# Single-head attention layers with the sources on the partitions, in groups of five destination blocks

## The chip, the cores and the metric
The kernel runs as one program on one core of a Trainium2 chip. The metric is the device time of one execution in microseconds. The core has a matrix engine (TensorE, PE in the profile), a vector engine (VectorE, DVE), a scalar engine (ScalarE, ACT), a general one (GpSimd, POOL), and queues that issue DMAs (SyncE, SP, above all). Each engine works through its own instructions in order and waits on semaphores for the others. SBUF and PSUM have 128 partitions; PSUM has eight banks of 2 KB a partition.

## The reference
A network over 3125 nodes of 256 features and 103125 edges (self loops among them): an attention layer of 8 heads of 32 columns, a mixture of experts, three single-head attention layers of 256 columns one after the other, and a last block that routes a part of the nodes. Each part adds to the node features. The three layers matter most here:

```python
def gat_conv(x, src, dst, W, a_src, a_dst, b):
    h = x @ W
    s = h @ a_src
    d = h @ a_dst
    alpha = jax.nn.leaky_relu(s[src] + d[dst], NEG_SLOPE)
    m = jax.ops.segment_max(alpha, dst, num_segments=n)
    ex = jnp.exp(alpha - m[dst])
    denom = jax.ops.segment_sum(ex, dst, num_segments=n)
    w = ex / (denom[dst] + 1e-16)
    out = jax.ops.segment_sum(h[src] * w[:, None], dst, num_segments=n)
    return out + b
x = jax.nn.gelu(gat_conv(x, src, dst, W1, as1, ad1, b1), approximate=False)
x = jax.nn.gelu(gat_conv(x, src, dst, W2, as2, ad2, b2), approximate=False)
x = jax.nn.gelu(gat_conv(x, src, dst, W3, as3, ad3, b3), approximate=False)
```

## The kernel before
The edge list is first turned into a dense mask in HBM, `mask_dram`, with a row for each destination and a column for each source: a large number where there is no edge, and otherwise what the count of equal edges adds to the score. From then on attention is dense. The nodes are 25 blocks of 128 (the last has 53), scores are kept negated, so that a maximum is a minimum, and everything is 4-byte floats.

The stages follow each other with no overlap: edges and mask (to 449 us), `heads_phase` (L821, to 1836), routing and experts (to 2316), `node_project_phase` (L1053, to 2366), `layers_phase` (L1229, to 3520), the last block. No planner and no scheduler orders the instructions: the order on an engine is the order of the code, and hand-offs are semaphore counts written by hand.

The heads run 200 units, one for each of 4 heads, 25 blocks and 2 passes. A unit is: DVE makes the scores of 128 destinations against 3125 sources (L978) and adds the mask with a running minimum (L982); ACT takes the exponentials in two halves, with their sums (L915); PE turns the 25 tiles of 128x128 so that sources lie on the partitions (L1014); ACT copies them from PSUM in four parts (L924); PE multiplies them with the sources' features (L1028). At a block's end ACT copies the sums out (L930), PE folds them (L1035), and ACT scales four pieces of 32 columns (L939) into the rows that POOL stores.

`node_project_phase` normalises the nodes and makes a table `hx` for the first layer (features of the sources and the two attention terms a node), and `el`, the source terms as a row on all partitions, plain and times 0.2.

The layers do for each destination block the same as a head's unit, with 256 columns: scores (L1309), mask and minimum (L1313), exponentials (L1487), 25 transposes (L1536), copies (L1496), 25 products with the stationary turned tile and 256 moving columns (L1547). Each turned tile waits for ACT's copy, each copy for PE's transposes, both with two buffers. A block behind, DVE divides by the sum and adds the bias (L1362), ACT takes the gelu (L1501), and for the next layer PE turns the row (L1557), projects it (L1566) and spreads its source term (L1574). The masks of the blocks come in one by one through two buffers on SP's queue (L1288), each when DVE is done with the one two blocks before.

Of the kernel before, what the change touches and what calls it, by code (L numbers as in the profile page):

```python
# [12 lines left out]
P = 128  # L13
# [399 lines left out]
def diagonal(g, first, rows, cols):  # L413

    flat = g["mask_dram"].rearrange("a b -> (a b)")
    start = first * (NS + 1)
    return flat[start:start + rows * cols * (NS + 1)].rearrange("(r q s) -> r q s", q=cols, s=NS + 1)[:, :, 0:1]
# [403 lines left out]
def heads_phase(nc, g, hx, el, mask, sc_first, nm, x1):  # L821

    with ExitStack() as ctx:
# [12 lines left out]
        psO = [ctx.enter_context(nc.psum_tensor(f"hd_psO{i}", [P, 512], F32)) for i in range(3)]  # L836
# [5 lines left out]
        s_mask = [sem(f"s_mask{i}") for i in range(2)]  # L842
        s_store = [sem(f"s_store{i}") for i in range(3)]
# [13 lines left out]

        @block.sync
        def _(sp):
            load_el(sp, 0, HG - 1, 0)  # L860
            load_el(sp, 0, HG - 1, 1)
            for B in range(2, BLOCKS):
                sp.wait_ge(s_nm, (B - 1) * HG)
                b = B % NB
# [4 lines left out]
                if b == 0:  # L869
                    for h in range(HG):  # L870
                        sp.wait_ge(s_lk, (B - 1) * HG + h + 1)
                        load_el(sp, B // NB, h, 0)
                        load_el(sp, B // NB, h, 1)

        @block.gpsimd
        def _(pool):
# [19 lines left out]
            for B in range(BLOCKS):  # L896
                q, b = B // NB, B % NB
                if B + 1 < BLOCKS:
                    halves_added(B + 1)
                pool.wait_ge(s_y, B + 1)  # L900
# [7 lines left out]
        def _(act):  # L908
# [17 lines left out]
            def copy_sums(B):  # L926
# [3 lines left out]
                nc.scalar.activation(oT[:, :, :].rearrange("p h n -> p (h n)"), psO[B % 3][:, 0:HG * P], ACT.Copy).then_inc(s_oT, 1)  # L930

            def rows(B):
                i = B % 3
                act.wait_ge(s_yT, B + 1)
                act.wait_ge(s_rd, B + 1)
                if B >= 3:
                    act.wait_ge(s_store[i], 16 * (B // 3))
                for h in range(HG):
                    last = nc.scalar.activation(y[:, i, h * CH:(h + 1) * CH], psY[:, h * CH:(h + 1) * CH], ACT.Copy,  # L939
                                                scale=rden[:, i, h:h + 1])  # L940
                last.then_inc(s_y, 1)

            exps(0, 0)
            exps(0, 1)
            for u in range(UNITS):
# [6 lines left out]
                for gi in range(4):  # L952
# [49 lines left out]
        def _(pe):  # L1002
# [14 lines left out]
            def products(n):  # L1017
# [3 lines left out]
                if gi == 0 and h == 0 and B >= 3:  # L1021
                    pe.wait_ge(s_y, B - 2)
                c0 = (B // NB * HG + h) * CH
                for t in range(TG[gi]):
# [3 lines left out]
                    last = nc.tensor.matmul(psO[B % 3][cg * CH:(cg + 1) * CH, h * P:(h + 1) * P], hx[0:r, tt, c0:c0 + CH],  # L1028
# [1247 lines left out]
```

## Time and profile before

| | us |
|---|---|
| Median of three runs | 3707.16 (3706.19 to 3713.21) |
| Profiled execution | 3711.51 |
| Its span in the profile | 3709.8 |
| PE busy in the span | 3419.7 |
| DVE busy | 2807.1 |
| ACT busy | 2515.5 |
| POOL busy | 316.0 |

The span is the time between the first and the last instruction that the profile shows of one execution. Busy times of an engine are sums over its instructions; instructions that follow each other closely overlap a little in the records, so that the distance of two starts says more of a price than a duration does. What the whole span hides, the stretches of the stages show.

### The profile page before, as it was taken

Reading aid. Unit: us, or ns where it says so; the run is one execution under the profiler, and the core shown is the slowest. Engines: PE = TensorE matmul, PEld = TensorE weight load, DVE = VectorE, ACT = ScalarE, POOL = GpSimd, SP = SyncE. Lnnn points to the kernel's source line nnn. Section 1 sums busy time; section 2 is a strip of 40 time slices with the busy share of each in tenths; the row PEclk is TensorE's granted clock in tenths of the full one; section 3 lists DMA queues with packets and bytes.
Section 4 is the critical chain, followed back from the end, with each engine's and each line's share of the span. In section 5 each row is a group of like instructions: output and inputs, shape, how many; then the busy total and the mean of one; then the engine's idle time right before and its main releaser. Section 6 shows DMA issues by size and latency. Waiting matters only on the chain. (4 is left out here: it accounts for less than half of the span.)

```text
span 3709.8 us, 69967 instructions
## 1 busy us (share of the span) xinstructions
PE 3419.7 (92%) x27369; PEld 2683.6 (72%) x27370; DVE 2807.1 (76%) x4237; ACT 2515.5 (68%) x4068; POOL 316.0 (9%) x280
## 2 busy tenths in 40 slices
PE   6999989999999999999769998799999999999999
PEld 4565566666666666666568998688878888888777
DVE  7999999999999999999652222766555565677594
ACT  5999899999999999999610111466656665676532
POOL 1000011010010010100004444000000000000000
PEclk9999999999999999999869999899999999999999
DMA  5433321121124211211268885322223221433101
GB/s 158 164 108 140 127 67 61 56 73 56 58 87 170 70 59 56 73 56 58 59 192 257 238 229 122 139 105 105 105 88 113 105 105 61 175 114 113 36 15 35
DMA packets 144871, 390.36 MB, mean 105 GB/s; under 512 B 20048, under 2 KB 91550, under 8 KB 126750
## 3 DMA queue, kind: packets, MB, share of 16 engines
q1 hardware_dynamic: 120520, 346.56, 26.7%
q0 software_dynamic: 20816, 36.07, 5.0%
q8 instruction: 224, 3.67, 0.4%
q10 hardware_dynamic: 3206, 3.20, 0.4%
q14 instruction: 105, 0.86, 0.1%
HBM read 327.87 MB, written 61.11 MB: 105 GB/s over the span
## 5 line engine op out<-in xcount | busy, mean ns | idle before, releaser
L924 ACT ACTIVATE hd_probsT<-hd_psT 128x768 f32<-128x768 f32 (+1 forms) x800 | 660.4, 852 | 70.2 <-PE hd_psT L1014 70.1
L1028 PE MATMUL hd_psO<-hd_probsT,hx 128*32 128x128 f32 (+1 forms) x10000 | 571.8, 281 | 129.1 <-ACT hd_probsT L924 129.0
L1547 PE MATMUL ly_psO<-hx_a,ly_probsT 128*128 128x256 f32 x2500 | 584.0, 381 | 0.0
L1028 PEld LDWEIGHTS hd_psO<-hd_probsT,hx 128*32 128x32 f32 (+1 forms) x10000 | 317.3, 108 | 322.6 <-ACT hd_probsT L924 216.0
L1496 ACT ACTIVATE ly_probsT<-ly_psT 128x768 f32<-128x768 f32 (+1 forms) x300 | 248.6, 829 | 393.6 <-PE ly_psT L1536 393.6
L1547 PEld LDWEIGHTS ly_psO<-hx_a,ly_probsT 128*128 128x128 f32 x2500 | 454.0, 189 | 71.4 <-issue 16.6
L1014 PE MATMUL hd_psT<-ident,hd_scores 128*128 128x128 f32 (+1 forms) x3325 | 478.9, 281 | 0.0
L978 DVE SCALAR_TENSOR_TENSOR hd_scores<-el_heads,hx 128x3125 f32<-128x3125 f32 x133 | 460.9, 3465 | 0.0
L982 DVE CUSTOM_DVE_ANT_0 hd_scores<-hd_scores,mask_heads 128x3125 f32<-128x3125 f32 x133 | 453.6, 3411 | 5.7
L915 ACT ACTIVATE hd_scores<-hd_scores,negmax 128x1664 f32<-128x1664 f32 (+1 forms) x266 | 430.1, 1617 | 5.4 <-DVE negmax L982 5.4
L1014 PEld LDWEIGHTS hd_psT<-ident,hd_scores 128*128 128x128 f32 (+1 forms) x3325 | 355.4, 141 | 98.9 <-issue 98.9
L1547 PE MATMUL ly_psO<-hx_b,ly_probsT 128*128 128x256 f32 x1250 | 292.7, 382 | 0.0
L489 DVE TENSOR_SCALAR onehot_c<-iotaC,stage_c 128x392 bf16<-128x392 f16 x1176 | 289.9, 316 | 0.0
L1536 PE MATMUL ly_psT<-ident,ly_scores 128*128 128x128 f32 x1875 | 258.2, 276 | 16.6 <-ACT ly_scores L1487 16.6
L2008 ACT ACTIVATE moe_hidden<-moe_ps_h 128x512 f32<-128x512 f32 x64 | 38.2, 597 | 331.7 <-PE moe_ps_h L1973 331.7
L1487 ACT ACTIVATE ly_scores<-ly_scores,ly_negmax 128x1664 f32<-128x1664 f32 (+1 forms) x150 | 239.3, 1595 | 22.0 <-DVE ly_negmax L1336 11.4
L1547 PEld LDWEIGHTS ly_psO<-hx_b,ly_probsT 128*128 128x128 f32 x1250 | 227.4, 190 | 35.8 <-issue 8.3
L1313 DVE CUSTOM_DVE_ANT_0 ly_scores<-ly_scores,ly_mask 128x3125 f32<-128x3125 f32 x73 | 248.9, 3410 | 3.1
L1014 PE MATMUL hd_psT<-ident,scores 128*128 128x128 f32 (+1 forms) x1675 | 243.1, 283 | 8.7 <-ACT scores L915 8.7
L1536 PEld LDWEIGHTS ly_psT<-ident,ly_scores 128*128 128x128 f32 x1875 | 221.2, 142 | 40.5 <-ACT ly_scores L1487 17.2
L1973 PEld LDWEIGHTS moe_ps_h<-moe_xT,moe_w 128*128 128x128 f32 x2048 | 241.5, 194 | 5.6 <-DVE moe_xT L2014 2.2
L1973 PE MATMUL moe_ps_h<-moe_xT,moe_w 128*128 128x128 f32 x2048 | 241.8, 277 | 1.6 <-DVE moe_xT L2014 1.6
(348 smaller groups left out, 5037.7 us busy)
## 6 DMA issues: line engine op xcount, KB each, us to landing
ly_mask<-mask_dram SPq DMA_DIRECT2D x72, 1568.0 KB, 6.6
moe_w<-in_L_ffn_w SPq DMA_DIRECT2D x144, 512.0 KB, 5.0
mask_heads<-mask_dram SPq DMA_DIRECT2D x46, 1568.0 KB, 6.7
mask_dram<-el_heads SPq DMA_DIRECT2D x196, 196.0 KB, 1.9
el_heads<-el_dram SPq DMA_DIRECT2D x5, 1568.0 KB, 9.7
el_heads<-el_slope_dram SPq DMA_DIRECT2D x5, 1568.0 KB, 13.1
x<-x SPq DMA_DIRECT2D x8, 640.0 KB, 8.4
el_heads<-el_dram POOLq DMA_DIRECT2D x3, 1568.0 KB
```

Of the source, the lines that this page charges most:

```text
L489: last = nc.vector.tensor_scalar(oc[:, k, :], g["iotaC"][:, :], c[:, k:k + 1], None, ALU.is_equal)
L915: nc.scalar.activation(sc[u % 3][:, halves[j]], sc[u % 3][:, halves[j]], ACT.Exp, scale=-1.0, bias=nm[:, u % 3:u % 3 + 1], accum_out=den[: ...
L924: nc.scalar.activation(pT[:, gi % 2, 0:w], psT[gi % 2][:, 0:w], ACT.Copy).then_inc(s_ev, 1)
L978: nc.vector.scalar_tensor_tensor(sc[c][:, :], el[:, h, 0, 0:N], hx[:, b, o:o + 1], el[:, h, 1, 0:N], ALU.subtract, ALU.min).then_inc(s_lk, 1)
L982: nc.vector.tensor_tensor_reduce(out=sc[c][:, :], in0=sc[c][:, :], in1=mask[:, B % 2, 0:N], scale=1.0, scalar=3.0e38, op0=ALU.add, op1=ALU ...
L1014: last = nc.tensor.transpose(psT[gi % 2][0:r, t * P:(t + 1) * P], sc[u % 3][:, c0:c0 + r], g["ident"][:, :])
L1028: last = nc.tensor.matmul(psO[B % 3][cg * CH:(cg + 1) * CH, h * P:(h + 1) * P], hx[0:r, tt, c0:c0 + CH], pT[0:r, gi % 2, t * P:(t + 1) * P ...
L1313: nc.vector.tensor_tensor_reduce(out=sc[:, c, :], in0=sc[:, c, :], in1=mask[:, B % 2, 0:N], scale=1.0, scalar=3.0e38, op0=ALU.add, op1=ALU ...
L1496: nc.scalar.activation(pT[:, gi % 2, 0:w], psT[gi % 2][:, 0:w], ACT.Copy).then_inc(s_ev, 1)
L1536: last = nc.tensor.transpose(psT[gi % 2][0:r, t * P:(t + 1) * P], sc[:, B % 3, c0:c0 + r], g["ident"][:, :])
L1547: last = nc.tensor.matmul(psO[B % 2][:, 0:D], pT[0:r, gi % 2, t * P:(t + 1) * P], hx[B // NB % 2][0:r, tt, 0:D], start=tt == 0, stop=tt == ...
L1973: last = nc.tensor.matmul(out[:, m * P:(m + 1) * P], w12[:, t % WS, i, k, m * P:(m + 1) * P], xT[:, t % 2, k, :], start=k == 0, stop=k == 1)
```

## The change
In the layers, scores are made with the sources on the partitions in the first place, so nothing is turned behind the exponentials. Five destination blocks form a group (640 columns). A group is 13 steps of two source tiles. In a step, DVE makes the scores of each tile from two rows that stand on all partitions (`rw`, one number a destination) and the tile's source term on the partitions (L1493), and adds a tile of the mask that lies turned in HBM, `maskT_dram` (L1503); ACT takes the exponentials (L1642); PE multiplies each 128x128 piece with the table, 257 columns, into the five PSUM banks of the five blocks (L1767). Column 0 of the table is 1, so that the sum of the weights falls out of the product. Four step buffers lie between DVE and PE (`RING`).

The maximum of a destination, needed before its scores can be shifted, comes from a pass over the untouched mask and `el` (L1510), one for each block of the next group, at the steps `at_step`; then a few short operations (`shifts`), spreads on PE (L1785) and copies on ACT (L1668) make the next group's two rows. At a group's end ACT drains the five banks (L1654) behind the exponentials of the next group's second step; DVE's division and ACT's gelu follow at its fourth; the former group's blocks are turned, projected and spread one by one between the products. In the layers' last group this is done after the last product, over all PSUM banks. In the last layer POOL adds the rows that DVE added before.

The heads turn the mask on the way: a quarter block a unit, three or four transposes on PE (`turn_mask`), a copy on ACT, a store by SP. One 128-column copy and a POOL multiplication take the place of ACT's four scaled pieces. The router's stage stores the diagonal to both masks and makes four weight columns more. The projection stage reads five masks (two before), and makes the first group's minima.

In the diff, `nm`, `sc` and the like are buffers, `s_...` semaphores.

```diff
 # heads
+            def store_turned(j):
+                sp.wait_ge(s_mc, j + 1)
+                sp.dma_start(g["maskT_dram"][...], mt[...]).then_inc(s_mst[j % 2], 16)
             for B in range(2, BLOCKS):
+                for h in range(HG - 1):
+                    store_turned((B - 2) * HG + h)
                 sp.wait_ge(s_nm, (B - 1) * HG)
+                sp.wait_ge(s_mT, (B - 1) * HG)
                 sp.dma_start(mask[0:r, B % 2, :], g["mask_dram"][b * P:b * P + r, :]).then_inc(s_mask[B % 2], 16)
...
-                for h in range(HG):
-                    last = nc.scalar.activation(y[:, i, h * CH:(h + 1) * CH], psY[:, h * CH:(h + 1) * CH], ACT.Copy,
-                                                scale=rden[:, i, h:h + 1])
+                nc.scalar.activation(y[:, i, :], psY[:, 0:P], ACT.Copy).then_inc(s_raw, 1)
...
+                    if gi == 3 and u + 2 < UNITS:
+                        copy_mask(u + 2)
                     if gi % 2 == 1 and u + 1 < UNITS:
                         exps(u + 1, gi // 2)
...
+                if n % 4 == 1 and n // 4 + 2 < UNITS:
+                    turn_mask(n // 4 + 2)
 # layers
+            def load_turned(C):
+                if C >= RING:
+                    sp.wait_ge(s_msk, C - RING + 1)
+                sp.dma_start(mT[0:r, s, 0:len(ks), 0:w], g["maskT_dram"][...])
+            for C in range(LAYERS * STEPS):
+                load_turned(C)
+                for B in fetch.get(C, ()):
+                    load_mask(B)
+            def scores(C):
+                if C >= RING:
+                    multiplied(dve, C - RING)
+                if c == 0:
+                    dve.wait_ge(s_row, spreads_upto(G) + SPREADS[G % NG])
+                for i, k in enumerate(tiles(c)):
+                    last = nc.vector.scalar_tensor_tensor(pb[0:r, s, i, 0:w], rw[0:r, G % 2, 0, 0:w], hx[l % 2][0:r, k, N8:N8 + 1],
+                                                          rw[0:r, G % 2, 1, 0:w], ALU.add, ALU.min)
+            def masked(C):
+                dve.wait_ge(s_mT[s], 16 * (C // RING) + 16)
+                nc.vector.tensor_tensor(pb[0:r, s, 0:n, 0:w], pb[0:r, s, 0:n, 0:w], mT[0:r, s, 0:n, 0:w], ALU.add)
+        at_step, first_steps = (0, 1, 2, 3, 5), (1, 2, 3, 5, 6)
+                    for c in range(NCK):
+                        if gi and c == 0:
+                            masked(C - 1)
+                        scores(C)
+                        if c:
+                            masked(C - 1)
+                        if gi + 1 < NG:
+                            maxima(first_of(G + 1) + d, G + 1)    # at its step
+                        if gi and c == 3:
+                            rows(G - 1)
 # ACT
+                        exps(G * NCK + c)
+                        if gi and c == 1:
+                            drain(G - 1)
+                        if gi and c == 3:
+                            gelus(G - 1)
 # PE, products of a step
+                pe.wait_ge(s_ex, C + 1)
+                for i, k in enumerate(tiles(c)):
+                    for d in range(size(G)):
+                        if k == 0 and G and d < size(G - 1):
+                            pe.wait_ge(s_dr, first_of(G - 1) + d + 1)
+                        nc.tensor.matmul(psO[d][0:m, 0:D + 1], pb[0:r, s, i, d * P:d * P + m], hx[l % 2][0:r, k, 0:D + 1], ...)
```

PE in the heads, one unit (`hd_psT` turned scores, `hd_psO` sums, `hd_psM` turned mask). Before:

```order
L1014 MATMUL hd_psT<-ident,hd_scores 128x128 x6
L1028 MATMUL hd_psO<-hd_probsT,hx 32x128 x6
L1014 MATMUL hd_psT<-ident,hd_scores 128x128 x5
L1014 MATMUL hd_psT<-ident,hd_scores 53x128
L1028 MATMUL hd_psO<-hd_probsT,hx 32x128 x6
```

And now:

```order
L1057 MATMUL hd_psT<-ident,hd_scores 128x128 x6
L1071 MATMUL hd_psO<-hd_probsT,hx 32x128 x6
L1089 MATMUL hd_psM<-ident,mask_heads 128x128 x3
L1057 MATMUL hd_psT<-ident,hd_scores 128x128 x5
L1057 MATMUL hd_psT<-ident,hd_scores 53x128
L1071 MATMUL hd_psO<-hd_probsT,hx 32x128 x6
```

The three mask tiles come between a unit's second products and its last transposes.

DVE in the first layer, one destination block of before (`ly_scores` scores, `ly_psX` and `ly_psH` the end of an earlier block):

```order
L1309 SCALAR_TENSOR_TENSOR ly_scores<-el,hx_a 128x3125
L1312 MEMSET ly_spare 1x1
L1313 ISA ly_scores,ly_negmax<-ly_scores,ly_mask 128x3125
L1313 ISA ly_negmax 128x1
L1317 TENSOR_SCALAR ly_has_edge<-ly_negmax 128x1
L1381 COPY x<-ly_psX 128x128
L1382 TENSOR_SCALAR x<-ly_psX 128x128
L1369 COPY ly_xT<-ly_psX 128x256
```

And now, from the last step of the first group to the third of the second (`probs` the four step buffers, `least` a block's minimum, `ly_mask` a mask by destinations):

```order
L1493 SCALAR_TENSOR_TENSOR probs<-ly_rows,hx_a 53x640
L1503 TENSOR_TENSOR probs<-probs,ly_mask_turned 128x1280
L1503 TENSOR_TENSOR probs<-probs,ly_mask_turned 53x640
L1493 SCALAR_TENSOR_TENSOR probs<-ly_rows,hx_a 128x640 x2
L1510 ISA ly_mask,least<-el,ly_mask 128x3125
L1510 ISA least 128x1
L1493 SCALAR_TENSOR_TENSOR probs<-ly_rows,hx_a 128x640 x2
L1503 TENSOR_TENSOR probs<-probs,ly_mask_turned 128x1280
L1510 ISA ly_mask,least<-el,ly_mask 128x3125
L1510 ISA least 128x1
L1493 SCALAR_TENSOR_TENSOR probs<-ly_rows,hx_a 128x640 x2
L1503 TENSOR_TENSOR probs<-probs,ly_mask_turned 128x1280
```

A new group's first scores are masked only behind the next step's scores and one minimum, its second step's behind two.

PE in the first layer, before, between one block's parts (`ly_psT` turned scores, `ly_psO` sums):

```order
L1536 MATMUL ly_psT<-ident,ly_scores 128x128 x7
L1547 MATMUL ly_psO<-hx_a,ly_probsT 128x256 x6
L1566 MATMUL ly_psH<-wx,ly_xT 128x258 x2
L1536 MATMUL ly_psT<-ident,ly_scores 128x128 x6
L1547 MATMUL ly_psO<-hx_a,ly_probsT 128x256 x7
L1574 MATMUL ly_psX<-ident,hx_b 128x128
```

And now in a group, around the spreads of the next group's rows (`ly_uv` to `ly_psR`):

```order
L1767 MATMUL ly_psO<-hx_a,probs 128x257 x30
L1796 MATMUL ly_psX<-ident,ly_sums 128x128 x2
L1767 MATMUL ly_psO<-hx_a,probs 128x257 x10
L1785 MATMUL ly_psR<-ident,ly_uv 128x128 x4
L1805 MATMUL ly_psH<-wx,ly_xT 128x260 x2
L1767 MATMUL ly_psO<-hx_a,probs 128x257 x10
L1796 MATMUL ly_psX<-ident,ly_sums 128x128 x2
L1815 MATMUL ly_psR<-ident,hx_b 128x128
```

Between products there are no turned scores any more, but the ends of the former group's blocks and the next group's rows.

## Rows read from the trace of the kernel before
**Rows 1.** Busy time of each engine by stretch; columns as in the first line
```profile
core 0: us, PE busy (x) PEld busy (x) DVE busy (x) ACT busy (x) POOL busy (x), PEclk, DMA share, GB/s
452.00:1830.00 1378.00, 1245.98 (x15400) 893.63 (x15400) 1354.88 (x846) 1296.26 (x1852) 127.51 (x104) 1.00 0.22 70
2372.00:3512.00 1140.00, 1124.85 (x6069) 960.33 (x6069) 701.71 (x1078) 708.16 (x832) 0.00 (x0) 0.99 0.30 104
2317.00:2333.00 16.00, 5.78 (x21) 4.42 (x22) 11.13 (x45) 1.83 (x6) 0.00 (x0) 0.54 1.03 358
2760.00:2765.00 5.00, 2.58 (x6) 1.37 (x5) 2.15 (x10) 0.44 (x1) 0.00 (x0) 0.50 0.00 0
2770.00:2775.00 5.00, 5.00 (x22) 4.23 (x22) 4.96 (x4) 2.47 (x4) 0.00 (x0) 0.79 0.55 176
```
**Rows 2.** The page's costliest groups, heads: busy us, mean ns | idle before, releaser
```profile
L924 ACT ACTIVATE hd_probsT<-hd_psT 128x768 f32<-128x768 f32 (+1 forms) x800 | 660.4, 852 | 70.2 <-PE hd_psT L1014 70.1
...
L978 DVE SCALAR_TENSOR_TENSOR hd_scores<-el_heads,hx 128x3125 f32<-128x3125 f32 x133 | 460.9, 3465 | 0.0
L982 DVE CUSTOM_DVE_ANT_0 hd_scores<-hd_scores,mask_heads 128x3125 f32<-128x3125 f32 x133 | 453.6, 3411 | 5.7
```
**Rows 3.** Timeline of DVE, heads and end of layers: start us, duration us
```profile
1001.73 3.41 DVE L982 CUSTOM_DVE_ANT_0 scores<-scores,mask_heads 128x3125 f32<-128x3125 f32 x1
...
1005.07 3.47 DVE L978 SCALAR_TENSOR_TENSOR hd_scores<-el_heads,hx 128x3125 f32<-128x3125 f32 x1
...
1008.58 3.41 DVE L982 CUSTOM_DVE_ANT_0 hd_scores<-hd_scores,mask_heads 128x3125 f32<-128x3125 f32 x1
...
3517.54 0.42 DVE L1416 SCALAR_TENSOR_TENSOR ly_y<-hx_b,ly_y 128x256 f32<-128x256 f32 x1
3517.88 0.42 DVE L1418 TENSOR_TENSOR x<-x,hx_b 128x256 f32<-128x256 f32 x1
```
**Rows 4.** Timeline of PE in the first layer, one block and a bit
```profile
2712.40 3.19 PE L1547 MATMUL ly_psO<-hx_a,ly_probsT 128*128 128x256 f32 x14
...
2716.30 2.75 PE L1547 MATMUL ly_psO<-hx_a,ly_probsT 128*128 128x256 f32 x12
2718.89 0.82 PE L1536 MATMUL ly_psT<-ident,ly_scores 128*128 128x128 f32 x6
...
2726.00 1.14 PE L1566 MATMUL ly_psH<-wx,ly_xT 128*128 128x258 f32 x4
2726.98 0.82 PE L1536 MATMUL ly_psT<-ident,ly_scores 128*128 128x128 f32 x6
2727.63 1.68 PE L1547 MATMUL ly_psO<-hx_a,ly_probsT 128*128 128x256 f32 x7
```
**Rows 5.** Waits of the layers: us in total, times, longest us
```profile
ACT ly_probsT L1496 <- PE ly_psT L1536: 393.6, 162, 3.6
```
**Rows 6.** Timeline of ACT in the heads and behind the last layer
```profile
1006.87 0.79 ACT L924 ACTIVATE hd_probsT<-hd_psT 128x768 f32<-128x768 f32 x1
1007.56 0.59 ACT L930 ACTIVATE hd_sumsT<-hd_psO 128x512 f32<-128x512 f32 x1
1008.03 0.81 ACT L924 ACTIVATE hd_probsT<-hd_psT 128x768 f32<-128x768 f32 x1
...
3512.34 1.28 ACT L1507 ACT_TABLE_LOAD   x1
```
**Rows 7.** Timeline of PE where the second layer follows the first
```profile
2755.70 1.14 PE L1566 MATMUL ly_psH<-wx,ly_xT 128*128 128x258 f32 x4
...
2766.38 3.03 PE L1536 MATMUL ly_psT<-ident,ly_scores 128*128 128x128 f32 x13 [3.29 <-ACT ly_scores L1487]
2769.21 4.66 PE L1547 MATMUL ly_psO<-hx_b,ly_probsT 128*128 128x256 f32 x14
```
**Rows 8.** POOL's sums in the heads: duration ns min/median/max
```profile
L887 POOL TENSOR_TENSOR hd_rden<-hd_den x50: 191/1700/3411, 474.5 to 1820.4; 128x4 f32<-128x4 f32 x50
```
**Rows 9.** The page's DMA issues: KB each, median us to landing
```profile
ly_mask<-mask_dram SPq DMA_DIRECT2D x72, 1568.0 KB, 6.6
```

More of the change, by code:

```diff
@@ L410, with diagonal @@
 LOOP_STEPS = -(-L1_LOOPS // DL)
[L413 to L415 removed]
+def diagonal(g, first, rows, cols, of="mask_dram"):
+    flat = g[of].rearrange("a b -> (a b)")
     start = first * (NS + 1)
@@ L1151, in _ @@
                 normalise(b)
-                if b > second.start:
-                    copy_h(b - 2)
-            copy_h(NB - 2)
-            copy_h(NB - 1)
-            dve.wait_ge(s_first_masks, 32)
+            dve.wait_ge(s_first_masks, 16 * len(places))
+            for i in range(len(PIECES)):
+                maxima(i)
+            n = len(places)
+            for i in range(1, len(PIECES)):
+                dve.wait_ge(s_least, (i + 1) * n)
+                c.wait()
+                c(nc.vector.tensor_tensor(qp[:, 0, :], qp[:, 0, :], qp[:, i, :], ALU.min))
+            c.wait()
+            c(nc.vector.tensor_copy(q[:, 0, 0:n], qp[:, 0, :]))
+            c.wait()
+        @block.gpsimd
+        def _(pool):
+            for table in tables:
+                nc.gpsimd.memset(table[:, :, 0:1], 1.0).then_inc(s_one, 1)
+            pool.wait_ge(s_one, len(tables))
         @block.scalar
@@ L1260, in layers_phase @@
-        ends = [min(e, NB) for e in LAST_GROUPS]
-        group_of = lambda e: range(ends[ends.index(e) - 1] if e != ends[0] else 0, e)
-        turned, upto = [], 0
-        for b in range(NB):
-            ready = max([e for e in ends if e + 2 <= b], default=0)
-            turned.append(range(upto, min(upto + 2, ready)))
-            upto = turned[-1].stop if turned[-1] else upto
-        late = range(upto, NB)
-        LAG = 4
-        added = [range(0) if b < LAG else range(LAG) if b == LAG else range(b - 1, b) for b in range(NB)]
@@ new lines, in layers_phase @@
+        tiles = lambda c: range(c * KC, min(c * KC + KC, NB))
+        depth = lambda k: min(P, N - k * P)
+        spreads_upto = lambda G: G // NG * sum(SPREADS) + sum(SPREADS[:G % NG])
+        place, user, landed = {}, {}, {}
+        latest, loads = [None] * len(masks), [0] * len(masks)
+        for B in range(LAYERS * NB):
+            if B < SIZES[0]:
+                s = B
+            elif B % NB in (2, 3):
+                s = B % NB
+            elif B % NB == SIZES[0] - 1:
+                s = UPPER
+            else:
+                s = 0 if latest[1] > latest[0] else 1
+            place[B], user[B] = s, latest[s]
+            latest[s] = B
+            loads[s] += 0 if B < SIZES[0] else 1
+            landed[B] = loads[s]
@@ new lines, in spread_rows @@
+            def spread_rows(G, j):
+                pe.wait_ge(s_uv, G + 1)
+                bank = psR if G % NG else psO[j]
+                if G % NG:
+                    pe.wait_ge(s_row, spreads_upto(G) + j)
+                if spread["el"]:
+                    pe.wait_ge(s_ec, spread["el"])
+                spread["rows"] += 1
+                for d in range(2 * j, min(2 * j + 2, size(G))):
+                    for i in range(2):
+                        o = (d - 2 * j) * 2 * P + i * P
+                        last = nc.tensor.matmul(bank[:, o:o + P], uv[:, G % 2, i, d:d + 1].broadcast_to([P, P]), g["ident"][:, :],
+                                                start=True, stop=True)
+                last.then_inc(s_sp, 1)
```

842 lines of the change are left out of this document (502 added, 340 removed).

## The prediction
> **What bounds the kernel now.** I read the busy time by stage first [rows 1]. In the heads stage (452 to 1830) DVE is busy 1354.88 of 1378 us, ACT 1296.26, PE 1245.98; in the layers stage (2372 to 3512) PE is busy 1124.85 of 1140, DVE and ACT some 705 each. So two stages with two limits. In the heads the page's groups confirm it: DVE's two passes over 3125 columns (L978, L982) stand idle 0.0 and 5.7 us in all, while ACT's copies of turned scores (L924) waited 70.2 us for PE [rows 2]. One head of one block costs DVE 3.34 + 3.51 = 6.85 us start to start [rows 3], and 199 of them are the stage. In the layers the waits show the reverse: ACT stood 393.6 us waiting for PE's transposes [rows 5]. One destination block there takes 2727.63 - 2712.40 = 15.23 us on PE without a gap [rows 4]. Of it, 25 products at 0.432 (each two instructions; 12 start within 2.59) are 10.8, 25 transposes at 0.109 (6 within 0.65) 2.7, and the end of a block (projection 0.98, two pairs of small transposes at 0.22) 1.42.
>
> **Heads.** Each unit gains three or four mask transposes on PE (0.11 each, 0.4), and on ACT a copy of 384 or 512 columns. ACT's prices start to start: 768 columns 0.69, 512 columns 0.47, so 0.86 ns a column and 384 cost 0.36 [rows 6]. ACT gives back four small scaled copies a block for one of 128 columns (some 0.8 to 0.15 a block, an estimate by the same line), 0.16 a unit. Net +0.22 on ACT. Its idle time was (70.2 + 5.4) / 199 = 0.38 a unit, and the new copy stands right before the exponentials whose following copies had that wait, so PE catches up in its shadow. DVE stays the limit: no change in cadence. If nothing of the wait is absorbed, ACT's unit is 6.85 + 0.22 - 0.1 at most, +22 us over the stage: rival C. The mask turning of units 0 and 1 delays PE's start some 2 us, but DVE needs the first unit's transposes only two units (13.7 us) later. The new stores (196 KB a unit) meet a stage whose DMA share is 0.22 [rows 1]. SP's mask loads now queue behind three stores of the block before; they have a block's 27 us for 6.6 us [rows 9]. The POOL multiplication of the last rows lies on the end: +1. I take +2, between 0 and 22.
>
> **Node projection and router.** The router's eight more tiny ACT copies and the second diagonal store lie beside waits: 0 (0 to 3). In the projection two masks become five, 7.8 MB at the 358 GB/s that 2317 to 2333 shows [rows 1]: 22 us, landed before the tables end. Five minima in four pieces are 5 x 3.34 plus 15 starts; only the last piece (two blocks, five short instructions) and the joins of 0.15 lie behind the last table: +4 (2 to 10). The layers give it back: they no longer begin with 6.85 us of DVE passes and an exponential of 1664 columns, but with four tiny DVE steps, ten spreads and three copies (5 us) and a first step (6 us). Equal.
>
> **Layers: work.** A group of five blocks is 13 steps. On PE a step is ten products, 4.34; a group 125 x 0.434 = 54.25, ten row spreads 2.2, five block ends 7.1: 63.5, against 5 x 15.23 = 76.2. All 25 transposes a block and ACT's copies behind them are gone. In the last layer blocks have no projection (15.23 - 1.42 + 0.22 = 14.03); 70.2 becomes 57.6. So PE alone would win 12.6 in 15 groups, 189 us.
>
> **Layers: what is late next.** DVE by its own starts: 256 columns 0.34, 3125 columns 3.34, thus 1.046 ns a column [rows 3]: 640 cost 0.74, 1280 cost 1.41. A step is 2 x 0.74 + 1.41 = 2.89; a step that also holds a block's minimum 6.23, more than PE's 4.34. A group is 13 steps (36.8), five minima (16.7), shifts and rows (3): 56.5 of PE's 63.5, so in the mean DVE keeps up, but the order matters. I added these durations in program order, with four slots between DVE and PE, 1.16 for two exponentials and 0.05 to 0.2 a hand-off:
> - First group: five steps with a minimum. PE waits 1.9 in steps 1 to 3, 0.5 and 2.8 in steps 5 and 6: 9.
> - Into the second group: its scores wait for rows spread after step 10. Then DVE does 1.48 + 3.34 + 1.48 + 1.41, ACT two exponentials, DVE 3.34 + 1.48 + 1.41, ACT two more, and only then (it stands behind the second exponentials) the drain that PE's first product waits for: about 15.5, of which PE covers steps 11 and 12 and little else. Behind the drain on ACT stand the exponentials of step 2, which PE does not want before it is through steps 0 and 1. PE waits 10, then 2.6 in the minima steps.
> - Into the third and fourth the rows come a step earlier and block ends fill PE: 3.1 + 1.5 each. Into the fifth, without minima: 2.2.
> Sum 33. PE works 5 x 63.5 less the last group's spreads and ends, 306: first to last product 339. Before: 25 x 15.23 less the last block's absent transposes, 378. Gain 39 in each of two layers. In the last layer there are fewer block ends to fill PE, boundaries cost 6.8 in place of 3.1, stalls 44 on 284: 328 against 348, gain 20.
>
> **Layer change.** Before, from the last projections (2755.70) to the next first product (2769.21) 13.5 us [rows 7]. After: drain 0.6, five rows 1.5, a table load 1.28 (row at 3512.34 [rows 6]), gelus to 4.6, five block ends at 1.31 of PE in a chain over ACT to 14.2, the last piece, joins and shifts 3, rows 4, first step 6: 27. Twice 13.5 lost. The tail has five blocks instead of one behind the last product: +3 (2 to 6).
>
> **Clock.** At the change before, the granted clock was 0.50 at 2760 to 2765 and still 0.79 at 2770 to 2775 [rows 1], and 14 products from 2769.21 are 4.66 long where 14 from 2712.40 are 3.19 [rows 4, 7]. Stalls of 10 us into three second groups and the longer changes should cost 2 to 3 each at 1.2 GHz: +8 (0 to 30, if the 3 us stalls do it too).
>
> **Sum.** Layers -(39 + 39 + 20) + 27 + 3 + 8 = -60; heads +2; projection +4. The profiled execution took 3711.51 (span 3709.8), so 3657; it lies 4.35 over the median 3707.16, so I forecast 3652.
>
> **Rivals.**
> A, the forecast: PE-bound with stalls at the group boundaries. Own range 3620 to 3690.
> B, fewer stalls: if half of the 110 us of stalls (33 + 33 + 44) is not there, because the four buffers cover more than my walk lets them: 3597. For it: DVE's mean is below PE's. Against: the boundary chain is a chain of data.
> C, the heads go over to ACT: 3652 + 20 = 3672. For it: ACT's margin is 0.38 - 0.22 a unit. Against: the wait it replaces.
> D, slower: late masks. In the layers SP now loads 655 KB of turned mask (rows of 2560 B) a step, and in the same queue the 1568 KB masks of the next group. Of blocks 3 to 5 of a group, each mask can start only when DVE has left the buffer two minima before, and is wanted 9.1 us later (6.23 + 2.89). In that time 2.2 MB must land; with 2 us of latency that asks 315 GB/s. The mean need is 16 MB in 65 us, 250 GB/s. Rows show 358 with 1 KB rows and 6.6 us for a mask alone [rows 1, 9], so it holds; below 315 it decides. At 200 GB/s a group's 16 MB take 81 us, 17 more than PE, in 15 groups: +250, and at 250 GB/s each of those three steps is some 3 late, +135 less what the stalls hide (half): 3720. That is the slower side.
> E, POOL against DVE. POOL's 50 small sums in the heads took 191 ns at best, 1700 in the median and 3411 at most [rows 8], the last one being the length of L982, and DVE's two passes have the same means with or without them. The change adds 50 multiplications of 128 columns in the heads and moves 50 additions of 256 to POOL in the last layer. If each held DVE for 0.4 us, twice POOL's shortest, the time would be 3652 + 40 = 3692. The Trainium skill ("SBUF — State Buffer", section "SBUF: two separate sides") says that a DVE operation with two SBUF inputs and a GpSimd operation that reads SBUF lock a shared port in turn for a whole instruction. By that rule the trace's waits of POOL agree (3411), but no row shows DVE paying, so it is a rival and no term.
>
> **Numbers.** A 0.58, B 0.10, C 0.10, D 0.14, E 0.08. Outcomes within 0.2% (7.4 us) cannot be told from no change. Faster than 3699.7: A but for 0.02, B, C and most of E, 0.80; same 0.06; slower 0.14, D. The range reaches to B below and to D's near end above: 3595 to 3715.
>
> **What would show it.** In the profile after: DVE's pair L1021 and L1025 in the heads still 6.85 apart and ACT's waits for PE below 70 us (C: DVE idle on turned scores). In the layers PE steps of 4.34, ACT hardly ever waiting for PE, PE waiting for exponentials most in the first product of second groups (about 10 us) and in first groups, DVE waiting for rows; no DVE wait of over 1 us for the masks (else D); DMA at 230 GB/s or more; some 27 us between layers with the clock at 0.50. Wrong if groups take 75 us or more, or if the heads grow by over 10.

## The result, and the profile after
The changed kernel took 3773.00 us (median of four, 3770.76 to 3776.33) against 3707.91 before: 65 us or 1.8% more by the medians; the ratio of the runs is on record as 1.0166, with an interval of 1.0144 to 1.0188. Forecast were 3652, with 3595 to 3715 as the range: wrong by 121 us, and on the other side of the kernel before. The profiled execution has a span of 3774.6 us, 64.8 more than before.

The first DMA issues of the stages show where the span went. The view is SP's timeline of the changed kernel; columns are start, length of a run of issues, and what they move.

```profile
1846.76 0.37 SPq L689 DMA_DIRECT2D gate_w<-in_L_ffn_gate_w  x1
...
2333.43 4.35 SPq L1151 DMA_DIRECT2D x<-x  x5
...
2389.54 1.54 SPq L1427 DMA_DIRECT2D ly_bias<-in_L_gnn_b  x3
...
3585.48 0.37 SPq L2326 DMA_DIRECT2D mod_w<-in_L_ffn_w  x1
```

| Stage | before | after | forecast |
|---|---|---|---|
| up to the end of the heads | 1836.6 | 1846.8 (+10.1) | +2 |
| routing and experts | 479.0 | 486.7 (+7.7) | 0 |
| node projection | 50.7 | 56.1 (+5.4) | +4 |
| layers | 1153.9 | 1195.9 (+42.0) | -60 |

Routing and experts run the same code but for the second diagonal and twelve small copies. From the first of the experts' 128 weight loads to the next stage it was 386.4 us before, 393.1 after, and 384.7 to 403.1 in the eleven runs below, which all leave it as it is. So these 7 us lie within the scatter of the profiled executions. The heads and above all the layers carry the error.

In the layers PE no longer stands at its limit. Busy time by layer, from the first to the last product (columns as in [rows 1]):

```profile
2403.50:2781.60 378.10, 338.68 (x1490) 275.00 (x1490) 274.02 (x289) 138.46 (x247) 0.00 (x0) 0.92 0.60 208
2811.30:3182.40 371.10, 335.12 (x1490) 272.50 (x1490) 272.38 (x289) 138.67 (x248) 0.00 (x0) 0.93 0.59 203
3212.20:3572.00 359.80, 311.25 (x1370) 249.84 (x1370) 290.77 (x361) 149.21 (x240) 51.18 (x40) 0.93 0.56 189
```

Where before PE was busy 1124.85 of 1140 at a granted clock of 0.99 [rows 1], it is now busy some 0.9 of each layer (0.87 in the last), at 0.92 or 0.93. The layers are 378, 371 and 357 long (the third window runs 2.9 us past the last product); forecast were 339, 339 and 328. ACT, which waited 393.6 us for PE [rows 5], now waits for DVE. The waits of the layers (total us, times, longest):

```profile
ACT probs L1642 <- DVE probs L1503: 299.7, 85, 12.0
...
PE ly_psO L1767 <- ACT probs L1642: 76.3, 25, 8.6
PE ly_psO L1767 <- ACT ly_sums L1654: 67.6, 12, 10.2
...
DVE ly_mask L1518 <- ACT el L1686: 35.4, 3, 14.2
DVE ly_mask L1518 <- ACT x L1686: 33.1, 3, 11.6
DVE ly_mask L1510 <- DMA ly_mask<-mask_dram: 28.6, 4, 9.0
```

The third row is the boundary between groups as the walk had it: twelve waits, longest 10.2, 67.6 in all; the forecast adds up to some 65 (63 to 66, as the last layer's fifth group is read). The last three rows are waits of DVE; but for those of the last piece at each layer change, the walk did not have them. They are where the search began. Two of them on DVE's timeline, in the fourth group of the first layer and at the fourth step of the fifth:

```profile
2629.72 1.48 DVE L1503 TENSOR_TENSOR probs<-probs,ly_mask_turned 128x1280 f32<-128x1280 f32 x1
2640.16 3.42 DVE L1510 CUSTOM_DVE_ANT_0 ly_mask<-el,ly_mask 128x3125 f32<-128x3125 f32 x1 [8.96 <-DMA ly_mask<-mask_dram]
...
2703.28 1.33 DVE L1503 TENSOR_TENSOR probs<-probs,ly_mask_turned 128x1130 f32<-128x1130 f32 x1
2716.17 2.16 DVE L1518 CUSTOM_DVE_ANT_0 ly_mask<-x,ly_mask 128x1920 f32<-128x1920 f32 x1 [11.55 <-ACT x L1686]
```

And PE's timeline around the end of that fourth group shows a difference of price:

```profile
2694.06 4.50 PE L1767 MATMUL ly_psO<-hx_a,probs 128*128 128x257 f32 x20
2698.40 1.04 PE L1805 MATMUL ly_psH<-wx,ly_xT 128*128 128x260 f32 x4
...
2710.44 4.96 PE L1767 MATMUL ly_psO<-hx_a,probs 128*128 128x257 f32 x20
2715.33 0.49 PE L1815 MATMUL ly_psR<-ident,hx_b 128*128 128x128 f32 x2
2715.66 4.97 PE L1767 MATMUL ly_psO<-hx_a,probs 128*128 128x257 f32 x20
2724.94 1.65 PE L1767 MATMUL ly_psO<-hx_a,probs 128*128 128x257 f32 x3 [4.31 <-ACT probs L1642]
```

A step of the fourth group starts 4.34 us before what follows it, as forecast; in the fifth group it is 4.89, with the granted clock at 1.00 (2702 to 2712) and nothing waited for. The last row's wait of 4.31 is the 11.55 us of DVE, come through the four buffers.

### The profile page after: what moved, and what is told of

It is laid out like the page before. It is cut to its first block and busy times, and to the rows that moved or that the text cites. A ratio compares the mean times of both kernels' runs of the same rounds, so it can differ in the third digit from the quotient of the medians.

```text
span 3774.6 us, 68675 instructions
## 1 busy us (share of the span) xinstructions
PE 3381.0 (90%) x26419; PEld 2613.9 (69%) x26420; DVE 2994.5 (79%) x4222; ACT 2316.3 (61%) x4102; POOL 457.5 (12%) x382
## 5 line engine op out<-in xcount | busy, mean ns | idle before, releaser
L1767 PE MATMUL ly_psO<-hx_a,probs 128*128 128x257 f32 (+1 forms) x2500 | 607.1, 399 | 101.5 <-ACT probs L1642 52.0
L960 ACT ACTIVATE hd_probsT<-hd_psT 128x768 f32<-128x768 f32 (+1 forms) x800 | 662.3, 852 | 38.2 <-PE hd_psT L1057 37.9
L1767 PEld LDWEIGHTS ly_psO<-hx_a,probs 128*128 128x128 f32 (+1 forms) x2500 | 476.8, 196 | 214.3 <-ACT probs L1642 113.9
L1767 PE MATMUL ly_psO<-hx_b,probs 128*128 128x257 f32 (+1 forms) x1250 | 303.9, 399 | 42.7 <-ACT probs L1642 24.4
L1642 ACT ACTIVATE probs<-probs,hx_a 128x640 f32<-128x640 f32 (+3 forms) x250 | 189.9, 809 | 218.8 <-DVE probs L1503 218.6
L1493 DVE SCALAR_TENSOR_TENSOR probs<-ly_rows,hx_a 128x640 f32<-128x640 f32 (+3 forms) x250 | 212.7, 891 | 120.4 <-PE ly_psO L1767 81.1
L1767 PEld LDWEIGHTS ly_psO<-hx_b,probs 128*128 128x128 f32 (+1 forms) x1250 | 239.0, 197 | 96.7 <-ACT probs L1642 46.7
L1503 DVE TENSOR_TENSOR probs<-probs,ly_mask_turned 128x1280 f32<-128x1280 f32 (+3 forms) x195 | 274.0, 1411 | 1.7 <-DMA ly_mask_turned<-mask_turned_dram 1.7
L2261 ACT ACTIVATE moe_hidden<-moe_ps_h 128x512 f32<-128x512 f32 x64 | 38.2, 597 | 338.7 <-PE moe_ps_h L2226 255.1
L550 PE MATMUL cnt<-onehot_c,onehot_dst_a 128*128 128x392 bf16 x1176 | 232.1, 334 | 11.3 <-DVE onehot_c L489 11.0
L918 POOL TENSOR_TENSOR hd_rden<-hd_den 128x4 f32<-128x4 f32 x50 | 100.4, 2008 | 1127.0 <-ACT hd_scores L951 737.4
```

Of the source, the lines that this page charges most:

```text
L550: last = nc.tensor.matmul(o, ohA[:, s, :, k], ohC[:, s, k, :], start=k == 0 and not further, stop=True, skip_group_check=True)
L960: nc.scalar.activation(pT[:, gi % 2, 0:w], psT[gi % 2][:, 0:w], ACT.Copy).then_inc(s_ev, 1)
L1493: last = nc.vector.scalar_tensor_tensor(pb[0:r, s, i, 0:w], rw[0:r, G % 2, 0, 0:w], hx[l % 2][0:r, k, N8:N8 + 1], rw[0:r, G % 2, 1, 0:w], ...
L1503: nc.vector.tensor_tensor(pb[0:r, s, 0:n, 0:w], pb[0:r, s, 0:n, 0:w], mT[0:r, s, 0:n, 0:w], ALU.add).then_inc(s_msk, 1)
L1767: last = nc.tensor.matmul(psO[d][0:m, 0:D + 1], pb[0:r, s, i, d * P:d * P + m], hx[l % 2][0:r, k, 0:D + 1], start=k == 0, stop=k == NB - 1)
```

## The experiments
The theory from these rows: four separate causes, each visible in one of the rows above (the last block's narrow tiles, the late masks, the partial minima's wait, and DVE's two minima at a boundary). The rivals: one common limit (DVE's sum, the DMA, the clock). All runs are the changed kernel with one edit unless said otherwise; times are medians, against 3773.0; lengths of the layers stage against 1195.9. Two runs that leave the layers as they are have 1195.6 and, with PE kept busy, 1195.3.

**Full tiles in the last block.**

```diff
-                        m = min(P, w - d * P)
+                        m = P
```

> The last block of a layer has 53 destinations; here its products use all 128 columns of the stationary tile instead of 53 (the surplus sums belong to no node and are not used). In the changed kernel a step of the last group takes 5.0 us on PE and of the other groups 4.34. Theory (switching between a 128-column and a 53-column stationary tile costs PE time, two such tiles a step): the step falls to 4.34, 8 us in each of three last groups, 20 to 26 us in all, near 3749. Rival (the 565-column rows of that group are slow in themselves, or DVE sets the step): no change, 3773.

3749.87 us (3748.73 to 3751.27); layers 1174.5, 21.4 shorter. PE's timeline in the fifth group of the first layer:

```profile
2703.22 4.50 PE L1767 MATMUL ly_psO<-hx_a,probs 128*128 128x257 f32 x20
2707.55 0.38 PE L1815 MATMUL ly_psR<-ident,hx_b 128*128 128x128 f32 x2
2707.77 4.50 PE L1767 MATMUL ly_psO<-hx_a,probs 128*128 128x257 f32 x20
```

The step is back at 4.33. More columns in the stationary tile made the step cheaper, and the sums for nodes that don't exist cost nothing.

**Narrow tiles side by side.** Does the change between tile shapes cost, or the narrow tile?

```diff
-                for i, k in enumerate(tiles(c)):
-                    for d in range(size(G)):
+                pairs = [(i, k, d) for i, k in enumerate(tiles(c)) for d in range(size(G))]
+                narrow = lambda d: w - d * P < P
+                for i, k, d in sorted(pairs, key=lambda p: narrow(p[2])):
...
```

> The last group's two products a step with a 53-column stationary tile stand side by side at the end of the step instead of each behind four full ones. Theory (the cost is in changing between tile shapes): half as many changes, the step falls from 5.0 to 4.7 us, 4 us a layer, 3761. Rival (a product with 53 columns is slow in itself): the step stays at 5.0, 3773.

3760.49 us (3755.15 to 3763.01); layers 1184.9, 11.0 shorter. PE in the same place:

```profile
2709.81 4.63 PE L1769 MATMUL ly_psO<-hx_a,probs 128*128 128x257 f32 x20
2714.37 0.49 PE L1817 MATMUL ly_psR<-ident,hx_b 128*128 128x128 f32 x2
```

4.56 to the next instruction, where it was 4.89 and is 4.33 with full tiles: of the excess of 0.56 a step, 0.23 is left with half of the changes. That answers to the switching theory; two narrow tiles side by side are as narrow as before. The rows of the weight loads (PEld) show the changes themselves. In the changed kernel a step holds two such pairs of pauses, one into the narrow tile and one out of it:

```profile
2712.26 0.17 PEld L1767 LDWEIGHTS ly_psO<-hx_a,probs 128*53 128x53 f32 x2 [0.33 <-issue]
2712.83 1.60 PEld L1767 LDWEIGHTS ly_psO<-hx_a,probs 128*128 128x128 f32 x8 [0.40 <-issue]
```

With the narrow tiles side by side it holds one pair, and with full tiles none:

```profile
2713.37 0.61 PEld L1769 LDWEIGHTS ly_psO<-hx_a,probs 128*53 128x53 f32 x4 [0.33 <-issue]
2714.37 0.30 PEld L1817 LDWEIGHTS ly_psR<-ident,hx_b 128*128 128x128 f32 x2 [0.40 <-issue]
```

**The burst of masks later.** Three masks of the next layer, 4.7 MB, came in one burst at the start of the fourth group, ahead of the mask that DVE wanted next.

```diff
-                return (B // NB) * STEPS - 2 * NCK + 3
+                return (B // NB) * STEPS - 2 * NCK + 9 + B % NB - 2
```

> The three masks of the next layer's first group that SP loads in one burst (4.7 MB) at the start of the fourth group come 6 to 8 steps later. In the changed kernel DVE waited 9.0 and 7.9 us for a mask in just these two groups, and their length was 77 us against 69 of the group before. Theory (late masks, of my rival D, at this place only): these waits go and both groups fall by some 8 us, 16 in all, 3757. Rival (the masks are late because the queue is full all the time): the waits appear at another mask, 3773.

3750.48 us (3746.69 to 3755.38); layers 1174.7, 21.2 shorter, a little over the expected 16. The waits for masks:

```profile
DVE ly_mask L1510 <- DMA ly_mask<-mask_dram: 11.8, 2, 7.2
```

Two of four waits are gone, the two at the starts of the first and the last layer are left, and none came up elsewhere: the queue is not full, it was asked in the wrong order.

**Partial minima later.**

```diff
-                        elif l < LAST and c in range(3, 3 + 2 * SIZES[0], 2):
+                        elif l < LAST and c in (5, 7, 9, 11, 12):
...
```

> In the last group of the first two layers, DVE takes its partial minima for the next layer (1920 columns) at steps 5, 7, 9, 11, 12 instead of 3, 5, 7, 9, 11. In the changed kernel the first of them waited 11.6 us for a copy of source terms that PE makes only behind the products of step 1, and the masking of step 3 stands behind it. Theory: PE's stall of 4 us (and a clock drop) in step 3 of these two groups goes, 5 to 8 us each, 10 to 16 in all, near 3760. Rival (the four buffers already cover it, PE loses nothing): 3773.

3762.25 us (3761.26 to 3770.07); layers 1181.5, 14.4 shorter. PE runs 60 products' instructions without a gap where it stood 4.31 us before:

```profile
2722.78 14.97 PE L1767 MATMUL ly_psO<-hx_a,probs 128*128 128x257 f32 x60
```

**The drain earlier.**

```diff
-                        if gi and c == 1:
+                        if gi and c == 0:
                             drain(G - 1)
```

> ACT empties the five sums behind the first exponentials of the next group instead of behind the second, one DVE step (6.3 us) earlier. Theory (DVE's chain of scores, mask and minima sets the first steps of a group; the drain is only the visible end of it): PE starts a group up to 6.3 us earlier but then waits for exponentials in steps 1 to 5; 1 to 3 us in each of 12 boundaries, 10 to 35 in all, near 3750. Rival (the wait for the drain is the loss itself): 6.3 us in each second group and in the last layer's groups, 3 in the others, 55 or more, with the clock staying up: 3715.

3758.08 us (3755.79 to 3775.59); layers 1183.4, 12.5 shorter. The waits change their name:

```profile
PE ly_psO L1767 <- ACT probs L1642: 122.9, 36, 12.8
...
PE ly_psO L1767 <- ACT ly_sums L1654: 14.6, 11, 3.8
```

53 us less are waited for the drain, and 47 more for exponentials. So the drain was the end of DVE's chain more than a cause of its own: of 53 us, 12.5 were gained.

**No minima at a boundary.**

```diff
-        shift_step = lambda G: 6 if G % NG == 1 else 5
+        shift_step = lambda G: 6 if G % NG == 1 else 4
...
-                maxima_at[B] = ((G - 1) * NCK + (first_steps if G % NG == 1 else at_step)[d]) if G % NG else G * NCK
+                early = (8, 10, 12, 15, 17) if G % NG == 2 else (7, 9, 11, 15, 17)
+                maxima_at[B] = G * NCK if G % NG == 0 else (G - 1) * NCK + first_steps[d] if G % NG == 1 else (G - 2) * NCK + early[d]
...
```

> The minima of the third, fourth and fifth groups are spread: three of them in steps 7, 9, 11 (8, 10, 12 in the first group) of the group two before, two in steps 2 and 4 of the group before; their shifts one step earlier. So no minimum stands between a group's first scores and its drain. Theory (the two minima there are the stall at the boundary): 6.7 us less DVE in front of the drain; second groups 7, others 3 to 6 earlier, 35 to 45 us in all, near 3733. Rival (DVE's sum or the masks' landing sets the groups, wherever the minima stand): 10 at most.

3725.37 us (3717.53 to 3729.76); layers 1146.1, 49.8 shorter, more than expected. The waits for the drain halve, and of the four waits for masks two are left:

```profile
PE ly_psO L1769 <- ACT probs L1644: 60.9, 22, 9.1
...
PE ly_psO L1769 <- ACT ly_sums L1656: 34.4, 12, 4.4
...
DVE ly_mask L1511 <- DMA ly_mask<-mask_dram: 11.9, 2, 7.1
```

A mask is fetched by the step of the minima before it in its buffer (`fetch_at`), so this edit moved the loads too, and the two late masks of the fourth groups are gone here as they are with the later burst. So not all of the 49.8 is the boundary: from first product to first product, the two fourth groups gave 16 of it.

**PE kept busy at a boundary.**

```diff
+                        if gi and c == 0 and l < LAST:
...
+                            for _ in range((0, 64, 20, 20, 12)[gi]):
+                                nc.tensor.transpose(psX[:, 0:P], g["ident"][:, :], g["ident"][:, :])
                         products(G * NCK + c)
```

> Added work whose result is not used: 64 transposes (7 us at full clock) on PE while it waits at the start of a second group, 20 at the third and fourth, 12 at the fifth, in the first two layers. Theory (the low clock behind a stall costs little here, since DVE sets the first steps): the granted clock stays up at the boundary, 0 to 6 us gained, near 3770. Rival (the clock is the large loss): 2 to 3 us at each of eight boundaries, 16 to 24, 3753.

3772.36 us (3766.09 to 3778.39), layers 1195.3: nothing. At these boundaries the granted clock did stay up; over the whole it rose only from 0.950 to 0.956, since it still fell in the first groups, at the layer changes and in the last layer, which the edit leaves as they are. Windows at the second group's start, of the changed kernel:

```profile
2480.00:2490.00 10.00, 1.25 (x3) 1.09 (x4) 10.00 (x7) 4.46 (x9) 0.00 (x0) 0.56 0.95 370
2490.00:2500.00 10.00, 10.00 (x36) 8.31 (x36) 9.93 (x16) 1.55 (x2) 0.00 (x0) 0.76 0.98 351
```

And of this one:

```profile
2480.00:2490.00 10.00, 8.13 (x69) 7.50 (x67) 10.00 (x9) 2.36 (x4) 0.00 (x0) 1.00 0.90 312
2490.00:2500.00 10.00, 8.85 (x41) 7.79 (x42) 9.93 (x12) 3.66 (x9) 0.00 (x0) 1.00 1.02 379
```

DVE is busy without a gap in both. At this place PE at 1.2 GHz lost what it would otherwise have waited for.

**POOL's operations made short.** They do 4 columns, and the kernel leaves out the others.

```diff
-                nc.gpsimd.tensor_tensor(rows_, rows_, rden[...].broadcast_to([P, HG, CH]), ALU.mult)
+                nc.gpsimd.tensor_tensor(rows_[:, :, 0:1], rows_[:, :, 0:1], rden[...], ALU.mult)
...
-                    nc.gpsimd.tensor_tensor(x[:, b, :], x[:, b, :], y_last[:, b, :], ALU.add)
+                    nc.gpsimd.tensor_tensor(x[:, b, 0:4], x[:, b, 0:4], y_last[:, b, 0:4], ALU.add)
...
```

> POOL's multiplication in the heads and its additions in the last layer do 4 columns in place of 128 and 256; the other columns are left without them. Theory (a POOL operation holds DVE's two-input passes up for its own length): the mean of DVE's mask pass in the heads falls from 3455 to 3415 and the stage by 8 to 10 us, and in the last layer DVE's additions lose their longest cases, 5 to 20 us there; together 13 to 30, near 3750. Rival (POOL waits and DVE does not, as I took the trace before): 0 to 3.

3759.55 us, with a wide spread (3748.60 to 3770.71); layers 1182.3, 13.6 shorter. DVE's mask pass in the heads (busy us, mean ns | idle), of the changed kernel:

```profile
L1025 DVE CUSTOM_DVE_ANT_0 hd_scores<-hd_scores,mask_heads 128x3125 f32<-128x3125 f32 x133 | 459.7, 3456 | 5.6
```

And of this one:

```profile
L1025 DVE CUSTOM_DVE_ANT_0 hd_scores<-hd_scores,mask_heads 128x3125 f32<-128x3125 f32 x133 | 454.1, 3414 | 5.7
```

42 ns less over 199 passes are 8.4 us of DVE. So POOL does hold DVE up; but the heads end only 3.4 us earlier (1843.4 for 1846.8), and what took the other 5 us no run separates. In the last layer the rows are plainer. DVE behind the scores of the third group, in the changed kernel:

```profile
3346.75 3.85 DVE L1510 CUSTOM_DVE_ANT_0 ly_mask<-el,ly_mask 128x3125 f32<-128x3125 f32 x1
...
3350.53 2.61 DVE L1493 SCALAR_TENSOR_TENSOR probs<-ly_rows,hx_a 128x640 f32<-128x640 f32 x2
```

And in this one:

```profile
3329.44 3.41 DVE L1510 CUSTOM_DVE_ANT_0 ly_mask<-el,ly_mask 128x3125 f32<-128x3125 f32 x1
...
3332.78 1.67 DVE L1493 SCALAR_TENSOR_TENSOR probs<-ly_rows,hx_a 128x640 f32<-128x640 f32 x2
```

PE's wait for the drain there falls from 9.3 to 7.1 us. The last layer is 10.5 us shorter from its first to its last product, and its tail 1.7.

**ACT scales the heads' rows again.**

```diff
...
-                nc.scalar.activation(y[:, i, :], psY[:, 0:P], ACT.Copy).then_inc(s_raw, 1)
+                for h in range(HG):
+                    last = nc.scalar.activation(y[:, i, h * CH:(h + 1) * CH], psY[:, h * CH:(h + 1) * CH], ACT.Copy,
+                                                scale=rden[:, i, h:h + 1])
...
```

> The heads' rows are scaled again by four ACT copies of 32 columns, as before the change; POOL's 50 multiplications of 128 columns are gone; the mask turning stays. In the changed kernel DVE's mask pass (3125 columns) took up to 3641 ns, mean 3455 against 3411, and the heads are 10 us longer. Theory (POOL's multiplication holds the port that DVE's two-input pass needs): the mean falls back to 3411, and the heads give back up to 9 us; ACT gains 0.23 us a unit where it stood idle 0.2 a unit, so part may come back: 3764 to 3773. Rival (the mask turning on PE and ACT makes the heads longer): mean back or not, the stage stays at +10, 3773 or more.

3801.29 us (3792.28 to 3810.68): slower by 28, past the theory's range, and with the heads at +34 where the rival had +10. The mask pass is back at 3410 ns, but the heads end 24 us later than in the changed kernel, and DVE now waits for PE's transposes, 23.0 us in all (the first row has two thirds of the units):

```profile
L1020 DVE SCALAR_TENSOR_TENSOR hd_scores<-el_heads,hx 128x3125 f32<-128x3125 f32 x132 | 457.6, 3467 | 16.6 <-PE hd_psT L1056 15.8 <-DMA el_heads<-el_slope_dram 0.2
...
L1024 DVE CUSTOM_DVE_ANT_0 hd_scores<-hd_scores,mask_heads 128x3125 f32<-128x3125 f32 x133 | 453.5, 3410 | 5.7
```

That is rival C, brought about by some 0.5 us of ACT a block (four copies are busy 0.82 together, the one copy 0.28), 0.13 a unit; 24 us over 200 units are 0.12. In the changed kernel the heads stand that close to it.

**Together.** The first five edits of the table below in one kernel.

> The full last block, the earlier drain, the later partial minima, the later burst of masks and the spread minima in one. Alone the first four gave 23, 15, 11 and 23 us. Theory (separate causes, but drain and spread minima share the boundary): 23 + 11 + 23 + 40 = 97, near 3676, faster than the kernel before by 30. Rival (a common limit, such as DVE's sum of 57 us a group or the DMA, takes over): 3700 or more.

3668.69 us (3667.16 to 3669.55), 0.9897 of the kernel before (0.988 to 0.9914): faster than both. Layers 1092.5, 103.4 shorter; the five gains one by one add up to 119.3, with the two late masks counted twice. PE's start into the second group, which was 10.16 us late, in the timeline of the changed kernel:

```profile
2488.75 1.62 PE L1767 MATMUL ly_psO<-hx_a,probs 128*128 128x257 f32 x3 [10.16 <-ACT ly_sums L1654]
```

And of this one:

```profile
2474.10 13.56 PE L1769 MATMUL ly_psO<-hx_a,probs 128*128 128x257 f32 x60 [0.50 <-ACT ly_sums L1656]
```

The two masks still waited for came earlier in a last kernel:

```diff
-            fetch.setdefault(max(fetch_at(B), RING - 1), []).append(B)
+            fetch.setdefault(0 if B < SIZES[0] + 2 else max(fetch_at(B), RING - 1), []).append(B)
...
-                if C == LAST * STEPS + RING:
+                if C == LAST * STEPS + NCK:
```

> The five edits together, and the two masks that DVE still waited for in them (7.2 us at the start of the first layer, 4.9 in the last) loaded earlier: the first behind one piece of the turned mask instead of four, the last layer's ahead of the node features, which come nine steps later. Theory (these waits are on the path of a first group, where DVE sets the pace): 8 to 12 less than the five edits alone (3668.7), near 3659. Rival (PE's cold start covers them): 3668.

3664.78 us (3661.57 to 3667.45), 0.9894 of the kernel before (0.9877 to 0.9910): 3.9 us less where 8 to 12 were expected, and not to be told from the 0.9897 without it. The masks' waits are gone, and turned masks are waited for instead:

```profile
DVE probs L1504 <- DMA ly_mask_turned<-mask_turned_dram: 7.7, 3, 5.2
```

| Edit | median | layers, against 1195.9 | expected of the whole |
|---|---|---|---|
| Full last block | 3749.9 | -21.4 | -20 to -26 |
| Earlier drain | 3758.1 | -12.5 | -10 to -35 |
| Later partial minima | 3762.3 | -14.4 | -10 to -16 |
| Later burst | 3750.5 | -21.2 | -16 |
| Spread minima | 3725.4 | -49.8 | -35 to -45 |
| PE kept busy | 3772.4 | -0.6 | 0 to -6 |
| Narrow tiles side by side | 3760.5 | -11.0 | -12 |
| Short POOL operations | 3759.6 | -13.6 | -13 to -30 with the heads |
| Five edits | 3668.7 | -103.4 | -97 |

## Why the prediction was wrong
**What held.** The bounds of the stages before; PE's step of 4.34 us; the heads as bound by DVE, with ACT's wait for PE falling as the copy took its place (70.2 us [rows 2] to 38.2); the projection, +5.4 for +4; the layer change, 29.7 us between products for 27; and the boundaries of the first two layers: PE waits 10.2, 3.0, 3.0 and 2.1 us for the drains, where the walk had 10, 3.1, 3.1 and 2.2. In the last layer two of them are 9.3 and 9.2, for 6.8.

**The step that failed is "Layers: what is late next".** Its sum of stalls, 110 us, was taken as all that PE loses beside its work, and the walk lacked four things (the first of them a price of the step before it, "Layers: work"). Their sizes are those of the runs:
- A price: all products were set at 0.434. The 53-column tile changes the shape on PE four times a step, 0.14 each, in 13 steps and three layers: 21 us.
- A queue: rival D had late masks, but priced them by the mean rate and the rows' rate, and asked only whether 315 GB/s can be had. The three masks of the next layer, issued in front of the one wanted, were in the code's fetch rule and not in the walk: 21 us. So D's mechanism was right in kind, at one place in two groups, and no matter of bandwidth.
- A wait: DVE's partial minima wait for the source terms of 15 blocks. The last of these comes behind PE's products of step 1, which wait for the drain. The walk has the fifth group "without minima" and no such wait: 14 us.
- A shared port: rival E, put at 40 us with a chance of 0.08, is real and smaller: DVE's passes in the heads are 8 us shorter without it, the heads themselves 3, and the layers 14, 12 of them in the last layer and its tail. The two parts together are measured as 13.4 us of the median, in runs that lie 22 us apart.

Together 70 of the 102 us by which the layers missed. Of the 8 by which the heads did, 3 came back without POOL's length; DVE's longer passes would account for all, but the rest stays open. Of the remaining 30 in the layers, longer scores (two of 640 columns 1.60 for 1.48), layer changes 3 longer each, a longer tail (16.4 us behind the last product, for 13.2 forecast) and two more late masks (7.1 us of DVE in the first group of the first layer, 4.7 in that of the last) explain a part by the trace. Only the masks were tried, on top of the five edits, and the 4 us that they gave lie within the spread; the rest stays open.

Two of its sums do not come out as written, and neither matters: PE's work in a layer is 308 us by its own terms and not 306, and four copies of 32 columns come to 0.23 us by the line it names and not 0.8 (ACT is busy 0.82 with them where a run brings them back, so the term stands).

Its own signs told against it: waits of DVE for masks of up to 9.0 us where none of over 1 was to be, groups of 77 us with 75 as the limit, heads longer by 10.1 with 10 as the limit, and 189 to 208 GB/s where it had 230 or more.

**The clock** was put at +8. The trace has it low in more places than that. Keeping it up at the boundaries of two layers gave 0.6 us: it was no cost there, where DVE set the pace. At the layer changes and in the last layer no run kept it up, so what it costs there stays open.

**The sign.** The forecast's gain of 55 us was a difference of 189 us saved on PE and some 130 lost in stalls and layer changes. All four things that the walk left out made it later. The chance of 0.14 for slower did not say so. That the five edits bring the layers to 1092.5 us, beside the forecast's 1094, is luck: two of them take away stalls at the boundaries that the forecast had counted in.

Of the port the trace says: DVE's mask pass in the heads grew from 3411 ns to 3641 at most, and in the mean by 44 x 199 / 50 = 175 ns for each of POOL's multiplications, whose usual length is 395 (min, median and max ns of the changed kernel):

```profile
L934 POOL TENSOR_TENSOR hd_y_stage<-hd_y_stage,hd_rden x50: 390/395/3642, 509.7 to 1837.6; 128x128 f32<-128x128 f32 x50
```

That is the lock that the Trainium skill states ("SBUF — State Buffer", section "SBUF: two separate sides"): whichever of a GpSimd operation that reads SBUF and a DVE operation with two SBUF inputs comes second waits. The trace agrees in kind: DVE pays part of a multiplication (231 ns at most), and POOL's maximum of 3642 is the other side of it.

## What to carry to other kernels
Before a step walk from durations is summed, go through every wait of each engine that it slows down, and through every queue in issue order: all that this one left out made it later. Where two engines come out within a tenth of each other, spread the second one's extra work evenly and keep it off the hand-over between groups: moving the minima was worth 50 us here, 16 of them by masks that came in time with it, and keeping the clock up there nothing. Pad an odd last tile to the full shape when it alternates with full ones: 21 us here. And a run that changes one thing can take a second with it: look whether the other waits are still there before its gain is put down to the first.

## What the runs showed of the hardware
A stationary tile of 53 columns among tiles of 128 makes PE slower and not faster: 0.28 us for each such product of 257 columns in 4-byte floats (4.89 for 4.33 us a step with two), 0.12 when two stand side by side. The weight loads pause 0.33 us before such a tile and 0.40 behind it. A GpSimd operation of 128 columns lengthened DVE's two-input pass beside it by up to 0.23 us. With PE's granted clock held at 1.00 over the stalls at the boundaries of two layers, the layers came out 0.6 us from those where it fell to 0.56 in one of them; DVE was busy without a gap in both.
